# A graph-attention kernel: edge gates transposed on VectorE in 32x32 blocks, bands of 1024 rows, all adjacency loads from SyncE

## The chip, the core and the metric

The kernel runs on one core of one Trainium2 chip. Its time is the device time of one execution in microseconds (us), the median of three runs. The core has TensorE (PE in the profile; PEld is its weight load), VectorE (DVE), ScalarE (ACT), GpSimd (POOL) and SyncE (SP), which here only issues transfers. A transfer (DMA) runs on the core's 16 DMA engines.

## The reference

One layer of graph attention over N = 8192 nodes with 128 features. The adjacency matrix is 8192 x 8192 int32, 268.4 MB, and is by far the largest input.

```
h = max(layernorm(x), 0);  Wh = h @ W
s1 = Wh @ a[:128];  s2 = Wh @ a[128:]
e = leaky_relu(s1[:, None] + s2[None, :], 0.2)
attention = softmax(where(adj > 0, e, -9e15), axis=1)
out = x + elu(attention @ Wh)
```

## The kernel before

**Stages.** A first stage loads x, normalises it, and builds `wh`: for each of 64 column tiles of 128 nodes, 128 partitions by 130 columns (the features, a one for the row sum, s1). Then the main loop goes over 16 bands of 512 rows. With a row factor and a column factor the softmax weight of row i and column j is `min(max(rbc[i], beta[j]), gate[i, j])`, where the gate byte is 1 for an edge and 0 for none, and a factor of the column is already multiplied into `wh`. This is the path that is taken when the spread of the scores is small (`safe_path`); the other path doesn't run on these inputs.

**One chunk** is 512 rows by 1024 columns, 2 MB of `adj`; there are 8 in a band and 128 in all. SP loads it with one transfer (`load`, L192) into one of 4 slots of `raw`: 128 partitions, 4 rows to a partition, runs of 4 KB. It may start when ScalarE has read the chunk that was in the slot (`gate_ready`). ScalarE turns it into bytes with `Sign` (`form_gates`, L407) into one of 2 slots of `gate`. TensorE transposes the gates, since the products need columns on the partitions: 16 transposes of 128x128 two-byte words into PSUM (`turn_gates`, L804). VectorE forms the weights for one column tile and 512 rows with one instruction (`steps`, L623), 8 to a chunk, reading the gate bytes from PSUM, into one of 4 slots of `weights`. TensorE multiplies (`multiply`, L814): 4 products of 128x128 by 128x129 in float32 to a step, each of which the trace shows as two passes; 4096 products, 8192 passes in all.

**Order.** Each engine has its own program, and they meet on semaphores. TensorE's program puts the transposes of the next chunk behind the fourth step of a chunk (`TURN_STEP`), in the same stream as the products. VectorE may be 4 steps ahead of TensorE (`weights_used`). The sums of a band are copied by ScalarE in the middle of the next band (L412), finished on GpSimd (L293 to L305, with one `Exp` on ScalarE), and stored by GpSimd's own queue (L307). For the next band TensorE spreads s1 over the partitions (`turn_s1`, L785) and VectorE and ScalarE make `rbc` (L572, L422). The last band is finished on VectorE (`last_band`) and stored by SP.

Of the kernel before, what the change touches and what calls it, by code (L numbers as in the profile page):

```python
# [13 lines left out]
P = 128  # L31
# [3 lines left out]
SAFE_SPREAD = 60.0  # L35

QUAD = 4
PACK = 2
ROWS = QUAD
CHUNK = 1024  # L40
STEPS = CHUNK // P
RAW_SLOTS = 4
GATE_SLOTS = 2
TURNED_SLOTS = 4
WT_SLOTS = 4
GROUP = QUAD
DVE_TILES = (1, 1, 2, 2)


def graph_attention(nc, x, adj, w, a, out):  # L50
    N, F = x.shape
    NT = N // P
    BANDS = N // (ROWS * P)
    BAND = ROWS * P
    CHUNKS = N // CHUNK
    GROUPS = NT // GROUP
# [5 lines left out]
    TURN_STEP = STEPS // 2 - 1  # L62
# [3 lines left out]
    QUADS = CHUNK // (QUAD * P)  # L66
    GATHER = QUAD
    assert F == P and CHUNKS % RAW_SLOTS == 0 and QUAD % WT_SLOTS == 0 and BANDS % 2 == 0
    assert len(DVE_TILES) == PER_PART

    with ExitStack() as ctx:
# [3 lines left out]
        def sem(name):  # L75
            return ctx.enter_context(nc.semaphore(name))

        raw = sb("raw", [P, RAW_SLOTS, ROWS, CHUNK], I32)
        gate = sb("gate", [P, GATE_SLOTS, ROWS, CHUNK], U8)
        xs = sb("xs", [P, NT, F])  # L80
        rbc = sb("rbc", [P, 2, BAND])
        wh = sb("wh", [P, NT, FE])
        s1_band = sb("s1_band", [P, ROWS])
        s2_all = sb("s2_all", [P, N])
        weights = sb("weights", [P, WT_SLOTS, BAND])
        hacc = sb("hacc", [P, 2, ROWS, FD])
        obuf = sb("obuf", [P, 2, ROWS, F])
        hp = sb("hp", [P, ROWS, F])
        neg = sb("neg", [P, ROWS, F])

        xn = weights[:, 0:2, :].rearrange("p s (t f) -> p s t f", f=F)
        ht = weights[:, 2:4, :]
        identf = sb("identf", [P, P])
        identb = sb("identb", [P, P], BF16)
        zeros = sb("zeros", [P, 2 * FD], BF16)
# [19 lines left out]
        empty = sb("empty", [P, 2, ROWS])  # L115
        rden = sb("rden", [P, 2, ROWS])
# [3 lines left out]
        acc = [ps[:, 2 * k:2 * k + 2, 0:2 * FD] for k in range(2)]  # L120
        wh_acc = [ps[:, 2 * k:2 * k + 2, 0:2 * FE] for k in range(2)]

        turned = [ps[:, 4 + k, :].bitcast(BF16).rearrange("p (c i) -> p c i", i=BAND) for k in range(TURNED_SLOTS)]
        turned_bytes = [ps[:, 4 + k, :].bitcast(U8).rearrange("p (c i b) -> p c i b", i=BAND, b=PACK)
                        for k in range(TURNED_SLOTS)]

        w_in, a_in = sem("w_in"), sem("a_in")  # L130
        x_in = [sem(f"x_in{k}") for k in range(4)]
        raw_in = [sem(f"raw_in{k}") for k in range(RAW_SLOTS)]
        out_done = [sem(f"out_done{k}") for k in range(2)]
# [9 lines left out]
        hmean_ready, mwh_done, mwh_ready = sem("hmean_ready"), sem("mwh_done"), sem("mwh_ready")  # L143
        ext_ready, gext_ready, flag_ready = sem("ext_ready"), sem("gext_ready"), sem("flag_ready")
        bias_ready = sem("bias_ready")

        s1_ready, s1_turned = sem("s1_ready"), sem("s1_turned")
        d_ready, z_ready, r_ready = sem("d_ready"), sem("z_ready"), sem("r_ready")
        w_first, w_rest = sem("w_first"), sem("w_rest")
        gate_ready = sem("gate_ready")  # L150
        turned_ready = sem("turned_ready")
        weights_ready = sem("weights_ready")
        weights_used = sem("weights_used")

        sums_copied = sem("sums_copied")
        hacc_free = sem("hacc_free")
        last_neg, last_exp, last_ready, last_out = (
            sem("last_neg"), sem("last_exp"), sem("last_ready"), sem("last_out"))
        rden_ready, neg_ready, exp_ready, out_ready = (
            sem("rden_ready"), sem("neg_ready"), sem("exp_ready"), sem("out_ready"))  # L160
# [3 lines left out]
        g_scores, g_probs = sem("g_scores"), sem("g_probs")  # L164
        g_turned, g_copied, g_used = sem("g_turned"), sem("g_copied"), sem("g_used")

        scores = raw[:, 2:4, :, :].rearrange("p s t j -> p (s t j)").bitcast(F32)
        adj_rows = raw[:, 0:2, :, :].rearrange("p s t j -> p (s t j)")
        x_blocks = x.rearrange("(k p b) f -> p k b f", p=P, b=QUAD)
        adj_blocks = adj.rearrange("(k p b) j -> p k b j", p=P, b=QUAD)  # L170
        out_blocks = out.rearrange("(k p b) f -> p k b f", p=P, b=QUAD)
# [9 lines left out]
        def _(sp):  # L181

# [3 lines left out]
            for load_of_x, (lo, hi) in enumerate([(0, PART // 2), (PART // 2, PART), (PART, 2 * PART), (2 * PART, NT)]):  # L186
                sp.dma_start(xs[:, lo:hi, :].rearrange("p (k b) f -> p k b f", b=QUAD),
                             x_blocks[:, lo // QUAD:hi // QUAD, :, :]).then_inc(x_in[load_of_x], 16)

            def load(band, chunk, slot):  # L190
                rows = adj_blocks[:, bass.ds(band, 1), :, chunk * CHUNK:(chunk + 1) * CHUNK]
                sp.dma_start(raw[:, slot, :, :], rows.rearrange("p k b j -> p (k b) j")).then_inc(raw_in[slot], 16)  # L192

            for k in range(RAW_SLOTS):
                load(0, k, k)

            def safe_path():

                for k in range(RAW_SLOTS, CHUNKS):
                    sp.wait_ge(gate_ready, k - RAW_SLOTS + 1)  # L200
                    load(0, k, k % RAW_SLOTS)
                with sp.Fori(1, BANDS) as band:
                    for k in range(CHUNKS):
                        sp.wait_ge(gate_ready, band * CHUNKS + (k - RAW_SLOTS + 1))
                        load(band, k, k % RAW_SLOTS)
                sp.wait_ge(last_ready, 1)
                sp.dma_start(out_blocks[:, BANDS - 1, :, :],
                             weights[:, 2, :].rearrange("p (b f) -> p b f", f=F)).then_inc(last_out, 16)
                sp.wait_ge(last_out, 16)

            def general_path():

                sp.wait_ge(gate_ready, 1)
                for k in range(RAW_SLOTS):
                    sp.wait_ge(raw_in[k], 16)
                with sp.Fori(0, BANDS) as k:
                    for b in range(QUAD):
                        sp.wait_ge(g_adj_free, k * QUAD + (b + 1))
                        sp.dma_start(adj_rows, adj_blocks[:, bass.ds(k, 1), b, :].rearrange("p k j -> p (k j)"))\
                            .then_inc(g_adj, 16)  # L220
# [10 lines left out]
        def _(pool):  # L231
            links = [0]

            def link(ins):

                links[0] += 1
                ins.then_inc(pool_chain, 1)
                pool.wait_ge(pool_chain, links[0])


            pool.sem_inc(hacc_free, 2)
            link(nc.gpsimd.memset(identf[:, :], 0.0))
            link(nc.gpsimd.affine_select(out=identf[:, :], in_=identf[:, :], compare_op=ALU.not_equal, fill=1.0,
                                         base=0, pattern=[[-1, P]], channel_multiplier=1))
            nc.gpsimd.tensor_copy(identb[:, :], identf[:, :]).then_inc(consts, 1)
            nc.gpsimd.memset(zeros[:, :], 0.0).then_inc(consts, 1)
            pool.sem_inc(consts, 1)
# [30 lines left out]
            LINKS = 4  # L278
            base = links[0]

            def finish_band(band, half, tiles, first, to, stored=None):

                done = [0]

                def chained(ins):
                    done[0] += 1
                    ins.then_inc(pool_chain, 1)
                    pool.wait_ge(pool_chain, band * LINKS + (base + done[0]))

                h, n, o = hp[:, 0:tiles, :], neg[:, 0:tiles, :], obuf[:, half, 0:tiles, :]  # L290
                row = [P, tiles, F]
                pool.wait_ge(rden_ready, band + 1)
                nc.gpsimd.tensor_tensor(n, empty[:, half, 0:tiles].unsqueeze(2).to_broadcast(row),  # L293
                                        mean_wh[:, :].unsqueeze(1).to_broadcast(row), ALU.mult)
                chained(nc.gpsimd.tensor_tensor(h, hacc[:, half, 0:tiles, 0:F],  # L295
                                                rden[:, half, 0:tiles].unsqueeze(2).to_broadcast(row), ALU.mult))
                chained(nc.gpsimd.tensor_tensor(h, h, n, ALU.add))  # L297
                pool.sem_inc(hacc_free, 1)
                nc.gpsimd.tensor_scalar(n, h, 0.0, None, ALU.min).then_inc(neg_ready, 1)  # L299
                chained(nc.gpsimd.tensor_scalar(h, h, 0.0, -1.0, ALU.max, ALU.add))  # L300
                if stored is not None:
                    pool.wait_ge(out_done[half], stored * 16)
# [6 lines left out]
            def finish_bands():  # L309
                def rows(band):  # L310
                    return out_blocks[:, bass.ds(band, 1), :, :].rearrange("p k b f -> p (k b) f")
# [607 lines left out]
```

## Time and profile before

| what | us |
|---|---|
| median of 3 runs (1108.24 to 1108.91) | 1108.8 |
| span of the profiled execution | 1107.6 |
| TensorE busy | 1077.9 |
| VectorE busy | 814.1 |
| ScalarE busy | 510.1 |
| GpSimd busy | 186.1 |

The span goes from the first to the last instruction of the profiled execution; a run's time has a little more around it. Busy time of matmuls is modelled, since they are pipelined; what a stretch of them costs is better read from the distance between their starts.

### The profile page before, as it was taken

To read this page: it belongs to the slowest core of one execution; us is meant where nothing else is said; L and a number is where in the kernel's file an instruction comes from. 1 tells how busy PE (TensorE), PEld (TensorE's weight loads), DVE (VectorE), ACT (ScalarE), POOL (GpSimd) and SP (SyncE) were. 2 spreads that over 40 slices of the span, in tenths; PEclk is the share of its full clock that TensorE was granted. 3 is DMA by queue.
4 is the path that set the end of the run, shared out by engine and by line. 5 is a ranking of instruction groups with operands and counts; after the bars stand their busy time and mean duration, and the time that the engine had idled before them with its cause. 6 is when DMAs were issued, how large, how long until landed. Compare 5 with 4: busy or idle time off the path is not lost.

```text
span 1107.6 us, 27993 instructions
## 1 busy us (share of the span) xinstructions
PE 1077.9 (97%) x10533; PEld 1072.1 (97%) x10533; DVE 814.1 (73%) x1249; ACT 510.1 (46%) x234; POOL 186.1 (17%) x168
## 2 busy tenths in 40 slices
PE   4799999999999999999999999999999999999997
PEld 4699999999999999999999999999999999999997
DVE  7677777777777777777777777777777777777776
ACT  3845435354453544544445444544454353544440
POOL 4340020110302012030200303020030202103030
PEclk9899999999999999999999999999999999999999
DMA  9596776776676767767677676676767767666700
GB/s 331 198 350 230 272 275 253 262 277 234 234 300 249 288 232 270 267 227 300 240 273 266 240 280 247 264 276 240 272 230 282 273 247 269 270 238 232 299 9 14
DMA packets 71499, 277.24 MB, mean 250 GB/s; under 512 B 2672, under 2 KB 2800, under 8 KB 71472
## 3 DMA queue, kind: packets, MB, share of 16 engines
q1 hardware_dynamic: 70272, 272.97, 64.9%
q0 software_dynamic: 1200, 3.93, 0.9%
q8 instruction: 15, 0.25, 0.1%
q14 instruction: 12, 0.10, 0.0%
HBM read 272.70 MB, written 4.19 MB: 250 GB/s over the span
## 4 chain that ended last, share of the span: by engine, by line
PE 94%; DVE 3%; issue 1%; DMA 0%; POOL 0%; POOLq 0%; ACT 0%; SPq 0%; DVEq 0%
PE ps L814 83%; PE ps L804 10%; DVE stats L490 1%; DVE weights L524 1%; PE ps L785 1%; PE ps L762 0%; PE ps L755 0%; DMA xs<-in_x 0%; PE ps L823 0%; DVE mean L507 0%; POOL wh L341 0%; DVE tmp L509 0%; DVE mean L505 0%; DVE weights L647 0%; DVE weights L642 0%
## 5 line engine op out<-in xcount | busy, mean ns | idle before, releaser
L623 DVE SCALAR_TENSOR_TENSOR weights<-rbc,beta,ps 128x512 f32<-128x512 f32 x1024 | 760.7, 747 | 271.0 <-PE ps L814 162.7
L814 PE MATMUL ps<-wh,weights 128*128 (+1 forms) x8192 | 949.8, 276 | 1.2 <-DVE weights L623 0.9
L814 PEld LDWEIGHTS ps<-wh,weights 128*128 128x128 f32 x8192 | 929.2, 192 | 2.1 <-issue 1.9
L407 ACT ACTIVATE gate<-raw 128x4096 uint8<-128x4096 int32 x127 | 459.0, 3615 | 442.5 <-PE ps L804 442.5
L804 PE MATMUL ps<-identb,gate 128*128 128x128 bf16 x2048 | 136.0, 220 | 1.8 <-DVE mean_wh L593 1.8
L293 POOL TENSOR_TENSOR neg<-empty,mean_wh 128x512 f32<-128x512 f32 x15 | 15.5, 1031 | 703.3 <-DVE rden L606 703.3
L804 PEld LDWEIGHTS ps<-identb,gate 128*128 128x128 bf16 x2048 | 125.9, 98 | 3.8 <-DVE mean_wh L593 2.2
L422 ACT ACTIVATE rbc<-rbc 128x512 f32<-128x512 f32 x16 | 10.1, 630 | 103.3 <-DVE rbc L572 103.3
L305 POOL TENSOR_TENSOR obuf<-obuf,neg 128x512 f32<-128x512 f32 x15 | 19.2, 1278 | 136.3 <-ACT neg L417 136.3
L300 POOL TENSOR_SCALAR hp<-hp 128x512 f32<-128x512 f32 x15 | 28.9, 1925 | 0.0
L755 PE MATMUL ps<-identf,weights 128*128 128x128 f32 x64 | 11.2, 302 | 13.5 <-POOL weights L262 9.5
L299 POOL TENSOR_SCALAR neg<-hp 128x512 f32<-128x512 f32 x15 | 22.5, 1500 | 3.1 <-POOL hp L297 3.1
L755 PEld LDWEIGHTS ps<-identf,weights 128*128 128x128 f32 x64 | 7.7, 154 | 15.6 <-issue 9.5
L303 POOL TENSOR_TENSOR obuf<-hp,xs 128x512 f32<-128x512 f32 x15 | 19.1, 1274 | 3.1 <-POOL hp L300 2.9
L297 POOL TENSOR_TENSOR hp<-hp,neg 128x512 f32<-128x512 f32 x15 | 19.1, 1270 | 1.2
L762 PE MATMUL ps<-wext,weights 128*128 128x130 f32 x128 | 17.8, 285 | 0.0
L762 PEld LDWEIGHTS ps<-wext,weights 128*128 128x128 f32 x128 | 16.4, 200 | 0.1
L341 POOL TENSOR_TENSOR wh<-wh,dcol x7 | 13.2, 1890 | 14.0 <-issue 13.7
L295 POOL TENSOR_TENSOR hp<-hacc,rden 128x512 f32<-128x512 f32 x15 | 15.5, 1031 | 0.0
L490 DVE BATCH_NORM_STATS2 stats<-xs 128x6 f32<-128x128 f32 x64 | 13.1, 280 | 2.3 <-DMA xs<-in_x 2.3
L259 POOL TENSOR_TENSOR weights<-xs,mean 128x384 f32 (+3 forms) x16 | 11.7, 730 | 13.6 <-DVEq L518 11.6
L447 ACT ACTIVATE weights<-weights 128x512 f32<-128x512 f32 x1 | 0.6, 630 | 26.8 <-DVE weights L650 26.8
(68 smaller groups left out, 151.6 us busy)
## 6 DMA issues: line engine op xcount, KB each, us to landing
raw<-in_adj SPq DMA_DIRECT2D x128, 2048.0 KB, 7.7
out_x<-obuf POOLq DMA_DIRECT2D x15, 256.0 KB, 2.4
xs<-in_x SPq DMA_DIRECT2D x1, 2048.0 KB, 12.9
xs<-in_x SPq DMA_DIRECT2D x2, 512.0 KB, 4.1
xs<-in_x SPq DMA_DIRECT2D x1, 1024.0 KB, 7.5
out_x<-weights SPq DMA_DIRECT2D x1, 256.0 KB, 2.2
wext<-in_L_gnn_W SPq DMA_DIRECT2D x1, 64.0 KB, 1.9
a<-in_L_gnn_a SPq DMA_DIRECT2D x2, 0.5 KB, 2.0
```

The lines of the kernel that those rows point to most:

```text
L297: chained(nc.gpsimd.tensor_tensor(h, h, n, ALU.add))
L299: nc.gpsimd.tensor_scalar(n, h, 0.0, None, ALU.min).then_inc(neg_ready, 1)
L300: chained(nc.gpsimd.tensor_scalar(h, h, 0.0, -1.0, ALU.max, ALU.add))
L303: chained(nc.gpsimd.tensor_tensor(o, h, xs[:, bass.ds(first, tiles), :], ALU.add))
L305: nc.gpsimd.tensor_tensor(o, o, n, ALU.add).then_inc(out_ready, 1)
L407: nc.scalar.activation(gate[:, k % GATE_SLOTS, :, :], raw[:, k % RAW_SLOTS, :, :], ACT.Sign).then_inc(gate_ready, 1)
L490: ins = nc.vector.bn_stats(stats[:, t, :].rearrange("p t s -> p (t s)"), xs[:, t, :].rearrange("p t s -> p (t s)"))
L623: nc.vector.scalar_tensor_tensor(weights[:, u % WT_SLOTS, :], rbc[:, half, :], beta[:, bass.ds(jt, 1)], turned_bytes[u // QUAD % TURNED_SL ...
L755: ins = nc.tensor.transpose(ps[:, 4 + slot, u * P:(u + 1) * P], xn[:, slot, u, :], identf[:, :])
L762: ins = nc.tensor.matmul(wh_acc[slot][:, u // 2, (u % 2) * FE:(u % 2 + 1) * FE], ht[:, slot, u * P:(u + 1) * P], wext[:, :], start=True, s ...
L804: ins = nc.tensor.transpose(turned[(k * QUADS + q) % TURNED_SLOTS][:, c, r * P:(r + 1) * P], words[:, c, :], identb[:, :])
L814: ins = nc.tensor.matmul(acc[half][:, r // 2, (r % 2) * FD:(r % 2 + 1) * FD], weights[:, u % WT_SLOTS, r * P:(r + 1) * P], wh[:, bass.ds(p ...
```

## The change

The gates are no longer transposed on TensorE. VectorE transposes them in blocks of 32x32 four-byte words, from SBUF to SBUF. A block transpose moves nothing between groups of 32 partitions, so the load has to put the rows and columns where the blocks need them.

- A band has 1024 rows (8 bands), a chunk is 1024 rows by 1024 columns (4 MB, 64 in all), loaded as two units of 2 MB (`load_unit`): 16 units in a band, 128 in all. The 4 slots of `raw` hold a unit each.
- A unit is loaded by four transfers of 512 KB, one for each group of 32 partitions, in the order 0, 2, 1, 3. Each partition takes 16 runs of 256 words (1 KB). `x` is loaded the same way, by 32 transfers (8 x 4) in place of 4. SP issues all of them.
- VectorE transposes a unit with one instruction of 128x1024 words, 2 in a chunk, behind its steps 3 and 6 and for the chunk that follows. A step forms 128x1024 weights, reads the gate bytes from SBUF, and multiplies by them instead of taking the minimum. TensorE has 8 products in a step.
- `rbc` is made from the transposed rows by ScalarE straight out of PSUM; `turn_z` takes the place of `turn_s1`. The share of rows without an edge comes in by three small bf16 products a band (`add_mean`).
- The sums are scaled by ScalarE from PSUM (`take_sums`: 16 small activations a band), finished on VectorE (`elu`, three instructions of 128x1024), and stored by SP, whose program waits for them between the loads of units 10 and 11 of the next band. GpSimd has no part in it any more.

```diff
-ROWS = QUAD
-CHUNK = 1024
+SQ = 32
+RUN = 256
+WORDS = RUN // QUAD
+WB = WORDS // SQ
+CHUNK = 4 * RUN
 STEPS = CHUNK // P
+BAND = CHUNK
+TILES = BAND // P
+UNIT = BAND // 2
+BLOCKS = UNIT // SQ
 RAW_SLOTS = 4
 GATE_SLOTS = 2
-TURNED_SLOTS = 4
...
+        g_o = [obuf[:, k * F:(k + 1) * F] for k in range(2)]
+
+
+        x_runs = x.rearrange("(k a w y b) f -> a k y w (b f)", a=4, w=WB, y=SQ, b=QUAD)
+        out_runs = out.rearrange("(k a w y b) f -> a y k w (b f)", a=4, w=WB, y=SQ, b=QUAD)
+
+        adj_runs = adj.rearrange("(k q w x b) j -> w x b k q j", q=4, w=WB, x=SQ, b=QUAD)
+        adj_tiles = adj.rearrange("(k a w y b) j -> a w b y k j", a=4, w=WB, y=SQ, b=QUAD)
+
+        def load_x(eng, k, group):
+            part = slice(group * SQ, (group + 1) * SQ)
+            eng.dma_start(xs[part, k * STEPS:(k + 1) * STEPS, :].rearrange("p (w b) f -> p w (b f)", b=QUAD),
+                          x_runs[group, k]).then_inc(x_in[k], 16)
+
+        def load_unit(eng, band, unit, groups):
+            chunk, half = unit // 2, unit % 2
+            slot = unit % RAW_SLOTS
+            for group in groups:
+                first = chunk * CHUNK + group * RUN
+                rows = adj_runs[half][:, :, bass.ds(band, 1), :, first:first + RUN]
+                eng.dma_start(raw[group * SQ:(group + 1) * SQ, slot, :, :].rearrange("p (b q) j -> p b q j", q=4),
+                              rows.rearrange("x b k q j -> x b (k q) j")).then_inc(raw_in[slot], 16)
...
+            for k in range(CHUNKS):
+                for group in (0, 2, 1, 3):
+                    load_x(sp, k, group)
+            for u in range(RAW_SLOTS):
+                load_unit(sp, 0, u, (0, 2, 1, 3))
...
+                    load_unit(sp, 0, u, (0, 2, 1, 3))
                 with sp.Fori(1, BANDS) as band:
-                    for k in range(CHUNKS):
-                        sp.wait_ge(gate_ready, band * CHUNKS + (k - RAW_SLOTS + 1))
-                        load(band, k, k % RAW_SLOTS)
-                sp.wait_ge(last_ready, 1)
-                sp.dma_start(out_blocks[:, BANDS - 1, :, :],
-                             weights[:, 2, :].rearrange("p (b f) -> p b f", f=F)).then_inc(last_out, 16)
-                sp.wait_ge(last_out, 16)
+                    for u in range(UNITS):
+                        sp.wait_ge(gate_ready, band * UNITS + (u - RAW_SLOTS + 1))
+                        load_unit(sp, band, u, (0, 2, 1, 3))
+                        if u == UNITS - 6:
+                            sp.wait_ge(out_ready, band)
+                            store_band(sp, band - 1, range(4), out_done)
+                for h in range(2):
...
+                def form_gates(band, u):
+                    turn = u // RAW_SLOTS + 1
+                    act.wait_ge(raw_in[u % RAW_SLOTS], band * (UNITS // RAW_SLOTS * 64) + turn * 64)
+                    if not isinstance(band, int) or band * UNITS + u >= GATE_SLOTS:
+                        act.wait_ge(turned_ready, band * UNITS + (u - GATE_SLOTS + 1))
+                    nc.scalar.activation(gate[:, u % GATE_SLOTS, :, :], raw[:, u % RAW_SLOTS, :, :], ACT.Sign)\
+                        .then_inc(gate_ready, 1)
...
                 def exp_rows(band, half):
-
-                    act.wait_ge(z_ready, band + 1)
-                    nc.scalar.activation(rbc[:, half, :], rbc[:, half, :], ACT.Exp, scale=SLOPE - 1.0)\
-                        .then_inc(r_ready, 1)
+                    act.wait_ge(z_turned, band + 1)
+                    nc.scalar.activation(rbc[:, half, :], zps.rearrange("p b i -> p (b i)"), ACT.Exp,
+                                         scale=SLOPE - 1.0).then_inc(r_ready, 1)
+
+                def take_sums(band, half):
+                    act.wait_ge(rden_ready, band + 1)
+                    if not isinstance(band, int) or band >= 1:
+                        act.wait_ge(out_ready, band)
+                    for t in range(TILES):
+                        rows, columns = slice(t * F, (t + 1) * F), acc[half][:, t // BANK_TILES, t % BANK_TILES, 0:F]
+                        scale = rden[:, half, t // BANK_TILES, t % BANK_TILES:t % BANK_TILES + 1]
+                        nc.scalar.activation(hbuf[:, rows], columns, ACT.Copy, scale=scale)
+                        ins = nc.scalar.activation(ebuf[:, rows], columns, ACT.Exp, scale=scale)
+                    ins.then_inc(sums_taken, 1)
+
+                def band_of_gates(band, half, first=False, last=False):
+                    for u in range(first, UNITS):
+                        form_gates(band, u)
+                        if u == 7 and not first:
+                            take_sums(band - 1, 1 - half)
+                        if u == 13 and not last:
+                            exp_rows(band + 1, 1 - half)
...
+                def turn_gates(band, u):
+                    dve.wait_ge(gate_ready, band * UNITS + (u + 1))
+                    words = gate[:, u % GATE_SLOTS, :, :].bitcast(I32).rearrange("p k (w y) -> p w k y", w=WB)
+                    half = u % 2
+                    nc.vector.transpose(turned[:, u // 2 % 2, :, half * UNIT:(half + 1) * UNIT], words)\
+                        .then_inc(turned_ready, 1)
+
+                def steps(band, half, pair, last=False):
+                    for u in range(PAIR):
+                        jt = pair * PAIR + u
+                        chunk, v = u // STEPS, u % STEPS
+                        if v == 0:
+                            dve.wait_ge(turned_ready, band * UNITS + pair * 4 + (2 * chunk + 2))
+                        dve.wait_ge(weights_used, band * BAND_STEPS + (jt + 1))
+                        nc.vector.scalar_tensor_tensor(
+                            weights[:, u % WT_SLOTS, :], rbc[:, half, :], beta[:, bass.ds(jt, 1)],
+                            turned_bytes[:, chunk, v // QUAD, :, v % QUAD], ALU.max, ALU.mult)\
+                            .then_inc(weights_ready, 1)
+                        if v in (3, 6) and not (last and chunk == 1):
+
+                            ahead = 2 * chunk + 1 + v // 3
+                            dve.wait_ge(gate_ready, band * UNITS + pair * 4 + (ahead + 1))
+                            words = gate[:, ahead % GATE_SLOTS, :, :].bitcast(I32)\
+                                .rearrange("p k (w y) -> p w k y", w=WB)
+                            to = slice((v // 3 - 1) * UNIT, v // 3 * UNIT)
+                            nc.vector.transpose(turned[:, 1 - chunk, :, to], words).then_inc(turned_ready, 1)
+
+                def reciprocals(band, half):
+
+                    dve.wait_ge(weights_used, band * BAND_STEPS + (BAND_STEPS + WT_SLOTS))
+                    nc.vector.reciprocal(rden[:, half, :, :], acc[half][:, :, :, F]).then_inc(rden_ready, 1)
+
+                def elu(band):
+                    def chained(k, ins):
+                        ins.then_inc(elu_chain, 1)
+                        dve.wait_ge(elu_chain, band * 2 + k)
+
+                    dve.wait_ge(sums_taken, band + 1)
+                    chained(1, nc.vector.tensor_scalar(ebuf, ebuf, 1.0, -1.0, ALU.min, ALU.add))
+                    chained(2, nc.vector.tensor_tensor(ebuf, ebuf, hbuf, ALU.max))
+                    if not isinstance(band, int) or band >= 1:
+                        dve.wait_ge(out_done, band * 64)
+                    nc.vector.tensor_tensor(
+                        obuf[:, :], ebuf, xs[:, bass.ds(band * TILES, TILES), :].rearrange("p t f -> p (t f)"), ALU.add)\
+                        .then_inc(out_ready, 1)
+
+                def band_of_weights(band, half, first=False, last=False):
+                    dve.wait_ge(r_ready, band + 1)
+                    if not last:
+                        z_of_band(band + 1)
+                    steps(band, half, 0)
+                    if not first:
+                        reciprocals(band - 1, 1 - half)
+                    steps(band, half, 1)
+                    if not first:
+                        elu(band - 1)
+                    if last:
+                        for pair in range(2, PAIRS):
+                            steps(band, half, pair, last=pair == PAIRS - 1)
+                    else:
+                        with dve.Fori(2, PAIRS) as pair:
+                            steps(band, half, pair)
...
+                def chunk_of_products(band, chunk, half, start=False, stop=False):
+                    pe.wait_ge(w_rest, chunk + 1)
+                    for u in range(STEPS):
+                        multiply(band, chunk, u, half, start and u == 0, stop and u == STEPS - 1)
+
...
+                def band_of_products(band, half, last=False, wait=True):
+                    if wait:
+                        pe.wait_ge(sums_taken, band - 1)
+                    chunk_of_products(band, 0, half, start=True)
+                    with pe.Fori(1, TURN_CHUNK) as chunk:
+                        chunk_of_products(band, chunk, half)
                     if not last:
-                        pe.wait_ge(sums_copied, band + 2)
-                        turn_s1(band + 1, 1 - half)
-                    with pe.Fori(PAIRS // 2, PAIRS - last) as pair:
-                        pair_of_chunks(pair)
-                    if last:
-                        for u in range(PAIR):
-                            if u == TURN_STEP:
-                                turn_gates(band, PAIRS - 1, 1)
```

## Rows read from the trace of the kernel before

**Rows 1.** The page: span, busy time and share of the engines
```profile
span 1107.6 us, 27993 instructions
PE 1077.9 (97%) x10533; PEld 1072.1 (97%) x10533; DVE 814.1 (73%) x1249; ACT 510.1 (46%) x234; POOL 186.1 (17%) x168
PE 94%; DVE 3%; issue 1%; DMA 0%; POOL 0%; POOLq 0%; ACT 0%; SPq 0%; DVEq 0%
```

**Rows 2.** Groups by line and shape: busy us, mean ns, idle before and releaser
```profile
L814 PE MATMUL ps<-wh,weights 128*128 x7936 | 920.5, 276 | 1.2 <-DVE weights L623 0.9 <-POOL wh L341 0.4
...
L804 PE MATMUL ps<-identb,gate 128*128 128x128 bf16 x2048 | 136.0, 220 | 1.8 <-DVE mean_wh L593 1.8
```

**Rows 3.** Chain that ended last: start us, length us, what
```profile
450.80 7.20 PE ps L814 x64
458.90 7.20 PE ps L814 x64
...
516.22 7.20 PE ps L814 x64
...
1088.09 11.68 PE ps L814 x104
```

**Rows 4.** Waits: who, for whom, us in total, times, longest
```profile
ACT gate L407 <- PE ps L804: 442.5, 110, 5.1
DVE weights L623 <- PE ps L814: 162.7, 192, 1.1
```

**Rows 5.** Groups by line and shape, VectorE and ScalarE
```profile
L623 DVE SCALAR_TENSOR_TENSOR weights<-rbc,beta,ps 128x512 f32<-128x512 f32 x1024 | 760.7, 747 | 271.0 <-PE ps L814 162.7 <-PE ps L804 0.8
L407 ACT ACTIVATE gate<-raw 128x4096 uint8<-128x4096 int32 x127 | 459.0, 3615 | 442.5 <-PE ps L804 442.5
...
L412 ACT COPY hacc<-ps 128x516 f32<-128x516 f32 x15 | 8.5, 570 | 0.0
...
L611 DVE TENSOR_TENSOR wh<-wh,dcol 128x1024 f32<-128x1024 f32 x1 | 1.2, 1226 | 0.2 <-issue 0.2
...
L642 DVE TENSOR_SCALAR weights<-ps,tmp 128x128 f32<-128x128 f32 x4 | 1.1, 346 | 0.0
...
L655 DVE SCALAR_TENSOR_TENSOR weights<-weights 128x512 f32<-128x512 f32 x1 | 0.7, 693 | 0.2 <-ACT weights L447 0.2
...
L650 DVE TENSOR_SCALAR weights<-weights 128x512 f32<-128x512 f32 x1 | 0.4, 427 | 0.0
```

**Rows 6.** Timeline where the main loop starts: start us, length us
```profile
47.49 0.15 DVE L590 TENSOR_SCALAR flag<-spread 128x1 int32<-128x1 f32 x1
...
50.90 2.72 DVE L623 SCALAR_TENSOR_TENSOR weights<-rbc,beta,ps 128x512 f32<-128x512 f32 x4 [0.81 <-PE ps L804]
```

**Rows 7.** Timeline of the end
```profile
1099.80 0.16 DVE L638 TENSOR_SCALAR tmp<-ps 128x4 f32<-128x4 f32 x1 [2.83 <-PE ps L814]
...
1104.66 0.37 SPq L207 DMA_DIRECT2D out_x<-weights  x1
```

**Rows 8.** The adjacency loads by line: issue ns (min/median/max), landing us
```profile
L192 SPq DMA_DIRECT2D raw<-in_adj x128: 539/543/5507, 4.3 to 1043.4; - x128
...
DMA to landing us min/median/max: 7.5/7.7/24.9
```

**Rows 9.** DMA in 20 to 34 us, 12 to 14 us and 4 to 10 us
```profile
DMA packets 1447, 5.73 MB, mean 410 GB/s; under 512 B 48, under 2 KB 48, under 8 KB 1446
...
DMA packets 400, 0.82 MB, mean 410 GB/s; under 512 B 0, under 2 KB 0, under 8 KB 400
...
DMA packets 1017, 2.01 MB, mean 334 GB/s; under 512 B 38, under 2 KB 38, under 8 KB 1017
```

More of the change, by code:

```diff
@@ L167, in graph_attention @@
+        adj_rows = raw[:, 0:2, :, :].rearrange("p s t j -> p (s t j)")
         scores = raw[:, 2:4, :, :].rearrange("p s t j -> p (s t j)").bitcast(F32)
[L168 to L171, printed above, removed]
+        g_hacc = [weights[:, k, UNIT:UNIT + FD] for k in range(2)]
@@ L173, in safe, with store_band @@
+        def store_band(eng, band, groups, signal):
+            for group in groups:
+                part = slice(group * SQ, (group + 1) * SQ)
+                rows = out_runs[group][:, bass.ds(band, 1), :, :].rearrange("y k w c -> y (k w) c")
+                eng.dma_start(rows, obuf[part, :].rearrange("p (w c) -> p w c", w=WB)).then_inc(signal, 16)
         def safe(eng):
@@ L276, in _ @@
                 .then_inc(gext_ready, 1)
-            LINKS = 4
             base = links[0]
[L281 to L302, printed above, removed]
-                chained(nc.gpsimd.tensor_tensor(o, h, xs[:, bass.ds(first, tiles), :], ALU.add))
-                pool.wait_ge(exp_ready, band + 1)
-                nc.gpsimd.tensor_tensor(o, o, n, ALU.add).then_inc(out_ready, 1)
-                pool.wait_ge(out_ready, band + 1)
-                pool.dma_start(to, o).then_inc(out_done[half], 16)
@@ L672, in safe_path @@
-                band_of_weights(0, 0)
+                for u in range(2):
+                    turn_gates(0, u)
+                band_of_weights(0, 0, first=True)
                 band_of_weights(1, 1)
@@ L845, in safe_path, with multiply @@
-                turn_gates(0, 0, 0)
+                def multiply(band, chunk, u, half, start, stop):
+                    pe.wait_ge(weights_ready, band * BAND_STEPS + chunk * STEPS + (u + 1))
+                    moving = wh[:, bass.ds(chunk * STEPS + u, 1), 0:FD].rearrange("p t f -> p (t f)")
+                    for t in range(TILES):
+                        ins = nc.tensor.matmul(acc[half][:, t // BANK_TILES, t % BANK_TILES, 0:FD],
+                                               weights[:, u % WT_SLOTS, t * P:(t + 1) * P], moving,
+                                               start=start and t % BANK_TILES == 0, stop=stop, skip_group_check=True)
+                    ins.then_inc(weights_used, 1)
@@ new lines, in band_of_products @@
+                def band_of_products(band, half, last=False, wait=True):
[4 more added lines that the diff above has]
+                        chunk_of_products(band, chunk, half)
+                    if not last:
+                        pe.wait_ge(r_ready, band + 1)
+                        turn_z(band + 1)
+                    with pe.Fori(TURN_CHUNK, CHUNKS - 1) as chunk:
+                        chunk_of_products(band, chunk, half)
+                    add_mean(half)
+                    chunk_of_products(band, CHUNKS - 1, half, stop=True)
@@ L846, in safe_path @@
                 pe.wait_ge(w_first, 2)
-                with pe.Fori(0, BANDS // 2 - 1) as pair:
+                for half in range(2):
+                    band_of_products(half, half, wait=False)
+                with pe.Fori(1, BANDS // 2 - 1) as pair:
                     for half in range(2):
```

480 lines of the change are left out of this document (212 added, 268 removed).

## The prediction

> **What bounds the kernel now.** I read the shares first: TensorE is busy 97% of the span and takes 94% of the chain that ended last, VectorE 73% [rows 1]. Of TensorE's time 8192 passes are products and 2048 are gate transposes; its waits for weights come to 1.2 us in all [rows 2]. VectorE and ScalarE wait for TensorE, 162.7 and 442.5 us [rows 4]. So TensorE's instruction stream is the limit, and the reader sees there what a chunk costs. The chain has a stretch of 64 passes every 8.09 us (450.80 to 458.90); the 64 take 7.20 us, 112.5 ns a pass, and the 16 transposes add 0.89 us, not the 1.06 that their busy time says. At the end 104 passes with no transpose among them take 11.68 us, 112.3 ns each, so the price holds without transposes too. A band takes 65.42 us (450.80 to 516.22), eight chunks and 0.70 us of its own [rows 3]. The loads are hidden: 2 MB land 7.7 us after issue [rows 8], and at 410 GB/s [rows 9] they occupy the DMA engines for 5.1 of the 8.09 us.
>
> **The change part by part.** The sum is made against the span, 1107.6 us; the median of the runs is 1.2 above it.
>
> TensorE. 128 times 16 transposes go: 128 x 0.89 = 114 us off the path. The passes stay 8192. The spreading of the row scores stays 64 transposes; 32 zeroing products become 24 wider ones. I count the 0.70 us of a band as unchanged for the same rows: 0. What is left is 7.20 us per 2 MB unit.
>
> VectorE is no longer covered as well. A step of 1024 columns from SBUF: the same operation took 693 ns for 512 columns, and 1024 columns of a two-input operation took 1226 ns [rows 5]; I take 1.23. No block transpose is in the trace. Bounds for 128x1024 words: twice the 427 ns of a one-input operation of 512 columns, 0.85 us, below, and two passes of the two-input one, 2.46 us, above; I take 1.23, the row with the same number of elements. A chunk is then 8 + 2 instructions, 12.3 us, against 14.4 us of products. `elu` adds 3 x about 1.1 us a band, which the four weight slots (up to 5 us of products ahead) cover. Nothing on the path. (The Trainium skill, page Vector Engine (DVE) Microarchitecture Reference, section 3.8 on the reshape front-end, has the block transpose sustain one element per cycle per lane; at its 0.96 GHz that would be 1.07 us plus a fixed part, and the sum would be the same. No run here shows it yet.)
>
> ScalarE: 16 gates of 3.62 us a band [rows 5], 16 activations of 128 columns (under 0.57 us each, the price of 516 columns), one `Exp` of 1024: under 69 of 115 us. Off the path.
>
> Start. Before, the first weights came 3.4 us after the flag, on one chunk's gates made in advance [rows 6]. Now the first step needs two units, and ScalarE makes the second after the flag (3.62 us), then VectorE transposes it: +4 us (0 to +10). End: last product to store issue took 4.9 us [rows 7]. Now 8 scalings at 0.28 to 0.35 us and two halves of three operations follow, and the store is split: +2 us.
>
> SP's program. `store_band` waits for `out_ready` between the loads of units 10 and 11, and loads 11 to 15 are queued behind it. `out_ready` comes after step 31 and `elu`. With VectorE three steps ahead and a step of 1.8 us, step 31 ends at 52 us of the band and `elu` at 55.6. Load 10 was issued when the gate of unit 6 was formed, at about 20.5 (unit 4 is transposed behind step 11, at 16.9, and the gate takes 3.6), so the DMA engines have nothing for 30 us. Four stores take 4 x 0.54 us to issue, load 11 goes out at 57.7, lands at 65.4, its gate is ready at 69.0, and its transpose was due behind step 38 at 64.2. Three steps of reserve cover all but 1 to 2 us; seven bands: +10 us (5 to 25).
>
> The loads. This decides. A unit is 2 MB in 7.20 us: 291 GB/s are wanted. The trace shows 410 GB/s, 25.6 per engine, at 4 KB packets and also at 2 KB packets, 334 where half-megabyte transfers follow each other [rows 9], always with all 128 partitions as the destination. That the rate doesn't depend on the packet says that each engine is held by a path in bytes. If the path is the engine's own, 32 partitions cost nothing: 410 is the bound above. If it belongs to the partitions, a transfer to 32 of them has its 16 engines, two partitions each, meet on fewer paths: half, 205 GB/s, is the bound that I take below. A second reason gives the same bound: should a 1 KB packet take the 80 ns that a 2 KB packet takes (400 in 2 us on 16 engines), the rate is 205 too. Groups 0 and 2 alternate, so engines that have drifted apart use different paths; but all start a transfer together and share evenly, and nothing drives them apart. I take 230, the lower bound and an eighth for such overlap.
>
> At 230 GB/s the loads set the end. x, `adj` and seven stored bands are 4.2 + 268.4 + 3.7 = 276.3 MB: 1201 us, starting at 4. Since DMA never idles in the first stage (12.6 MB are queued before the flag at 47.5), the gap before the main loop is used up. In each of seven bands the wait of SP for `out_ready` leaves the queue dry: after load 9 lands, 3.6 (gate) + 1.2 + 1.2 + 3.4 (transpose, step 31, `elu`) + 2.1 (stores) + 2 to the first byte is 13.5 us, against 9.1 for load 10: 4 x 7 = 28. After the last landing: gate 3.6, transpose 1.2, eight steps of products 14.4, end 10: 29. Together 4 + 1201 + 28 + 29 = 1262, with 1.2 around the span **1263 us**.
>
> The Trainium skill, page SBUF — State Buffer, section Door 1 (the DMA port swizzle), says that partitions 0 to 31 reach 8 of 16 ports, 189 GB/s at 1 MB against 328 for all partitions, 218 at best; its part on issuing two DMAs for both halves says that they serialize, 6% better than one. By 218 the sum would be 1329, by 6% more, 231 GB/s, 1258. No transfer of before goes to fewer partitions, so the trace can't say whether it agrees.
>
> **The rivals.**
> *Full rate.* The path is the engine's own and 1 KB packets cost by their bytes. For it: the same 25.6 GB/s per engine at two packet sizes. Against: no row with few partitions. At 334 GB/s or more a unit takes 6.3 us or less, under 7.20, TensorE stays the limit: 1107.6 - 114 + 4 + 2 + 10 = 1010, with 1.2 **1011 us** (995 to 1040). Faster. It decides from 291 GB/s up; between that and 264 the change still gains.
> *Partly shared.* The pairs drift apart by half a transfer: 410/1.5 = 273 GB/s, 276.3 MB in 1012 us, with 61 us around: 1074. For it: twelve hundred microseconds are long to drift. Against: engines that run dry start together again. Break-even is at 264 GB/s (1047 us of transfers).
> *VectorE becomes the bound.* The transpose takes the 2.46 us of its upper bound: a chunk is 8 x 1.23 + 4.92 = 14.8 against 14.4 us; with 3.7 us a band for `elu` and the sums, 64 x 14.8 + 8 x 3.7 = 977 in place of 922 + 6: at full rate 1011 + 50 = 1061. Against: 1.23 has the nearest row, and TensorE's stretch gives it 2 us a chunk of slack.
>
> **How the numbers follow.** Loads at 205 to 264 GB/s, 52%: 1110 to 1409 by the bounds, its own range 1120 to 1400, 1263 likeliest. Full rate 33%. Partly shared, about 255 to 291 GB/s, 11%: 6 faster, 2 within the bound, 3 slower. VectorE 4%. Faster by over 0.2% (about what a measurement of this kernel tells from no change): 33 + 4 + 6 = 43%. Within 0.2%: 2%. Slower: 52 + 3 = 55%. The range for 8 in 10 has to hold both signs: 1003 to 1385.
>
> **What would show it.** Right: TensorE's busy share falls to about 75%, the chain goes through DMA landings and ScalarE's gate, ScalarE's idle time is put down to `raw`, the DMA share is near 1.0 in nearly all slices while GB/s are near 230, and a packet of 1 KB takes 70 ns or more. Wrong: GB/s above 290 where loads are dense, a packet of 42 ns or less, TensorE at 7.20 us for 64 passes without gaps. The steps on SP: SP waits for VectorE's last `elu` instruction seven times, with no DMA in that time. The transpose of 128x1024 at 1.2 us; the step at 1.23; the first weights 7 us behind the flag. If VectorE is busy over 95% while TensorE waits for weights, it is the third rival.

## The result: 19% slower, and the loads set the time

The changed kernel takes 1319.5 us (median of 4 runs, 1313.2 to 1324.0) against 1108.9 us (4 runs, 1108.2 to 1109.8) before. The ratio is 1.190 with a 95% interval of 1.186 to 1.193. The forecast was 1263 us, by the case in which the loads become the limit; its own range was 1120 to 1400. The page and rows below are of the run of 1313.2 us.

The page of the changed kernel, to be read against [rows 1]: span, busy time, the clock, DMA and GB/s in 40 slices, and the chain that ended last by engine.

```profile
span 1311.6 us, 21997 instructions
PE 1049.4 (80%) x8477; PEld 1026.5 (78%) x8477; DVE 843.5 (64%) x825; ACT 523.8 (40%) x309; POOL 55.9 (4%) x63
...
DMA  8999999999999999999999999999999999999990
GB/s 222 223 225 222 223 223 221 220 197 216 215 218 217 202 223 223 221 223 196 218 219 217 205 211 221 221 220 198 223 224 225 223 200 222 222 222 222 200 207 18
...
q1 hardware_dynamic: 275760, 276.67, 106.1%
...
SPq 75%; DMA 9%; issue 6%; DVE 5%; ACT 3%; PE 2%; DVEq 0%; POOL 0%; ACTq 0%
```

TensorE fell from 97% busy to 80% and from 94% of the chain to 2%. The DMA engines are busy in every slice but the last and still move only 196 to 225 GB/s, where [rows 9] had 410. They are not idle, their packets are slow: 106.1% of 16 x 1311.6 us over 275,760 packets is 81 ns for one of 1 KB (a share above 100% says that the times of an engine's packets overlap a little).

The waits (engine, line, for whom: us in total, times, longest) answer to [rows 4].

```profile
ACT gate L409 <- DMA raw<-in_adj: 735.5, 125, 11.6
DVE big L604 <- ACT gate L409: 414.1, 111, 9.2
PE ps L801 <- DVE weights L593: 224.3, 88, 7.3
...
SPq L183 <- DVE obuf L621: 80.7, 7, 11.8
```

ScalarE waited for TensorE's transposes before; now it waits for a landing at 125 of its 127 gates, VectorE's transposes wait for ScalarE, TensorE waits for VectorE. The last line is SP waiting for the band's result, once in each of seven bands.

ScalarE's gates in order of time (start, length, what, idle before) show the pace of the units and one wait of SP. The last line below is the window around that wait (us, busy time of the engines, then the clock, the DMA share and GB/s).

```profile
745.14 3.62 ACT L409 ACTIVATE gate<-raw 128x4096 uint8<-128x4096 int32 x1 [6.04 <-DMA raw<-in_adj]
754.49 3.62 ACT L409 ACTIVATE gate<-raw 128x4096 uint8<-128x4096 int32 x1 [5.73 <-DMA raw<-in_adj]
768.94 3.62 ACT L409 ACTIVATE gate<-raw 128x4096 uint8<-128x4096 int32 x1 [10.83 <-DMA raw<-in_adj]
...
750.00:759.00 9.00, 5.62 (x48) 5.25 (x47) 8.80 (x9) 3.62 (x1) 0.00 (x0) 1.00 0.60 134
```

Between waits a gate follows the last one after 9.3 to 9.8 us in most cases (9.35 in the lines shown); a unit of 2.097 MB in 9.6 us is 218 GB/s, in 9.35 it is 224. Where SP waited the distance is 14.45 us, 4.8 to 5.1 more. Not all of that is lost: the band's store, 0.52 MB, falls into it. In the 9 us around the wait the DMA engines moved 134 GB/s, which at a pace of 221 is 3.5 us without work.

The compute side is as the forecast had it. These are the groups by line (busy us, mean ns, idle before).

```profile
L593 DVE SCALAR_TENSOR_TENSOR weights<-big,beta 128x1024 f32<-128x1024 f32 x512 | 634.1, 1289 | 23.7 <-PE ps L801 23.4
L604 DVE STREAM_TRANSPOSE big<-gate 128x1024 int32<-128x1024 int32 x126 | 156.8, 1244 | 414.2 <-ACT gate L409 414.1
```

### The profile page after: what moved, and what is told of

Read it like the earlier page. It is cut to its first block, busy times and chain, and to the rows that moved or that the text cites. A ratio compares the mean times of both kernels' runs of the same rounds, so it can differ in the third digit from the quotient of the medians.

```text
span 1311.6 us, 21997 instructions
## 1 busy us (share of the span) xinstructions
PE 1049.4 (80%) x8477; PEld 1026.5 (78%) x8477; DVE 843.5 (64%) x825; ACT 523.8 (40%) x309; POOL 55.9 (4%) x63
## 3 DMA queue, kind: packets, MB, share of 16 engines
q1 hardware_dynamic: 275760, 276.67, 106.1%
## 4 chain that ended last, share of the span: by engine, by line
SPq 75%; DMA 9%; issue 6%; DVE 5%; ACT 3%; PE 2%; DVEq 0%; POOL 0%; ACTq 0%
SPq L176 74%; DMA raw<-in_adj 8%; ACT gate L409 3%; PE ps L801 1%; SPq L183 1%; DVE stats L497 1%; DVE weights L593 1%; DVE big L618 1%; DVE obuf L621 1%; DVE weights L527 1%; DVE big L617 0%; PE ps L767 0%; DVE big L604 0%; DMA xs<-in_x 0%; SPq L208 0%
## 5 line engine op out<-in xcount | busy, mean ns | idle before, releaser
L801 PE MATMUL ps<-wh,weights 128*128 (+1 forms) x8192 | 1008.3, 288 | 231.7 <-DVE weights L593 224.3
L801 PEld LDWEIGHTS ps<-wh,weights 128*128 128x128 f32 x8192 | 990.0, 203 | 249.8 <-issue 198.2
L593 DVE SCALAR_TENSOR_TENSOR weights<-big,beta 128x1024 f32<-128x1024 f32 x512 | 634.1, 1289 | 23.7 <-PE ps L801 23.4
L604 DVE STREAM_TRANSPOSE big<-gate 128x1024 int32<-128x1024 int32 x126 | 156.8, 1244 | 414.2 <-ACT gate L409 414.1
L425 ACT ACTIVATE big<-ps,rden 128x128 f32<-128x128 f32 x56 | 23.3, 417 | 0.0
L424 ACT ACTIVATE big<-ps,rden 128x128 f32<-128x128 f32 x56 | 22.9, 409 | 0.0
L788 PE MATMUL ps<-identf,zband 128*128 128x128 f32 x64 | 12.4, 360 | 0.8 <-DVE zband L566 0.8
L387 ACT ACTIVATE weights<-ps 128x512 f32<-128x512 f32 x16 | 9.6, 598 | 6.3 <-PE ps L760 6.3
L527 DVE TENSOR_SCALAR weights<-xs,mean,rstd 128x128 f32<-128x128 f32 x24 | 10.2, 463 | 2.8 <-PE ps L760 2.8
L788 PEld LDWEIGHTS ps<-identf,zband 128*128 128x128 f32 x64 | 11.0, 191 | 1.0 <-DVE zband L566 1.0
L267 POOL TENSOR_TENSOR weights<-weights,rstd 128x384 f32<-128x384 f32 (+1 forms) x16 | 11.6, 725 | 2.2 <-POOL weights L264 1.4
```

Of the source, the lines that this page charges most:

```text
L424: nc.scalar.activation(hbuf[:, rows], columns, ACT.Copy, scale=scale)
L425: ins = nc.scalar.activation(ebuf[:, rows], columns, ACT.Exp, scale=scale)
L527: ins = nc.vector.tensor_scalar(xn[:, slot, u, :], xs[:, t, :], mean[:, t:t + 1], rstd[:, t:t + 1], ALU.subtract, ALU.mult)
L593: nc.vector.scalar_tensor_tensor(weights[:, u % WT_SLOTS, :], rbc[:, half, :], beta[:, bass.ds(jt, 1)], turned_bytes[:, chunk, v // QUAD, ...
L604: nc.vector.transpose(turned[:, 1 - chunk, :, to], words).then_inc(turned_ready, 1)
L788: ins = nc.tensor.transpose(zps[:, t // 4, t % 4 * P:(t % 4 + 1) * P], zband[:, t:t + 1].to_broadcast([P, P]), identf[:, :])
```

## The experiments

**Is it the 32 partitions? Two loads for the kernel before.** The first loads each chunk by four transfers of 32 neighbouring partitions, the second by four transfers of 32 partitions that lie four apart. All else is equal between them: the number and size of the transfers, packets of 4 KB, and how many partitions a transfer has. (The semaphore counts change to 64 to match; so in all runs with four transfers.)

```diff
-                sp.dma_start(raw[:, slot, :, :], rows.rearrange("p k b j -> p (k b) j")).then_inc(raw_in[slot], 16)
+                for group in (0, 2, 1, 3):                            # second run: range(4)
+                    part = slice(group * 32, (group + 1) * 32)        # second run: slice(group, P, 4)
+                    sp.dma_start(raw[part, slot, :, :], rows[part].rearrange("p k b j -> p (k b) j"))\
+                        .then_inc(raw_in[slot], 16)
```

> The kernel before, but each 2 MB chunk is loaded by four transfers of 32 neighbouring partitions in the order 0, 2, 1, 3, still in packets of 4 KB. Theory A (write paths belong to partitions, 32 neighbours reach half of them): 218 GB/s in dense stretches, 9.6 us a chunk against TensorE's 8.09, so the loads become the limit: about 14 + 128 x 9.6 + 12 = 1255 us. Theory B (a 1 KB packet costs nearly what a 2 KB packet costs): packets are 4 KB here, nothing changes, 1109. Theory C (transfers of 512 KB are too small): 334 GB/s or what the change showed, 218; by the former 1109, by the latter 1255, and then the next run tells it from A.

> As the run before, but each of the four transfers goes to 32 partitions four apart (0, 4, 8 ... then 1, 5, 9 ...). Same number of transfers, sizes, packets and partitions per transfer. Theory A: these 32 reach all write paths, 400 GB/s or more where loads are dense, 1109 us. Theory B: 1109. Theory C (size or number of transfers): the same time as the run with neighbouring partitions, 1255 if that one is slow.

Measured: 1237.8 us with neighbours, 1108.9 us with every fourth (before on the same chip: 1108.6; one run each). The page of the first and then of the second:

```profile
GB/s 255 226 228 229 229 234 225 225 233 224 233 225 225 231 223 231 225 225 232 224 233 225 233 224 224 232 224 232 225 225 233 225 233 226 233 225 228 237 231 41
...
q1 hardware_dynamic: 76416, 272.99, 99.5%
```

```profile
q1 hardware_dynamic: 76416, 272.99, 69.0%
```

Where the loads are dense at the start, from 20 to 34 us, the second moves 410 GB/s as the kernel before does [rows 9], and the first 224:

```profile
20.00:34.00 14.00, 10.31 (x85) 9.28 (x84) 13.47 (x54) 11.35 (x27) 10.32 (x15) 1.00 1.03 410
```

The same 76,416 packets take 257 ns each to neighbours (99.5% of 16 x 1236.1 us) and 160 ns to every fourth partition (69.0% of 16 x 1107.2). So neither the number of partitions nor the size of a transfer costs anything here; which partitions they are does. That is theory A: the limit in bytes belongs to groups of partitions, and 32 neighbours get little more than half of the full rate. The Trainium skill, page SBUF — State Buffer, section Door 1 (the DMA port swizzle), gives 8 of 16 ports and at best 218 GB/s for partitions 0 to 31. The traces agree on the half, but not on "at best": the changed kernel moves 215 to 225 GB/s in slices without a store, and this run 223 to 237 from its second slice on (the stores, 1.4% of the bytes, are in it). With the groups in the order 0, 1, 2, 3 it is 209 to 220 (the fifth experiment).

**Is it the 1 KB packet?** The kernel before with four transfers a chunk of all 128 partitions, each for 256 columns, so in packets of 1 KB. (A version with one transfer a chunk and 1 KB runs gave no result.)

```diff
+                for c in range(4):
+                    first = chunk * CHUNK + c * 256
+                    rows = adj_blocks[:, bass.ds(band, 1), :, first:first + 256]
+                    sp.dma_start(raw[:, slot, :, c * 256:(c + 1) * 256], rows.rearrange("p k b j -> p (k b) j"))\
+                        .then_inc(raw_in[slot], 16)
```

> The kernel before, each 2 MB chunk in four transfers of 128 partitions, one for each quarter of the columns: four transfers of 512 KB and packets of 1 KB, as in the changed kernel, but every transfer goes to all partitions. Theory A (write paths of the 32 partitions): 350 to 400 GB/s where loads are dense, a packet of 1 KB takes 41 to 47 ns, hidden behind TensorE, 1109 us, at most 1115. Theory B (cost of the 1 KB packet, or of 1 KB reads at the memory): 205 to 230 GB/s, 9.1 to 10.2 us a chunk, 1200 to 1330 us.

Measured: 1108.7 us against 1109.0. From its page, and its window from 20 to 34 us:

```profile
q1 hardware_dynamic: 273024, 272.99, 75.6%
...
20.00:34.00 14.00, 10.41 (x85) 9.38 (x84) 13.57 (x56) 11.44 (x27) 10.61 (x16) 1.00 1.10 349
```

A packet took 49 ns (75.6% of 16 x 1107.0 us over 273,024), against 81 in the changed kernel. A quarter of the length costs 0.31 of the 160 ns above: by a straight line through the two, an estimate, the fixed part is some 12 ns. It isn't free, since the dense stretch has 349 GB/s in place of 410, but it is far from the half, and theory B falls. The memory's layout is not the same here (rows 32 KB apart in turn, not also 8 MB apart), so for that part only the next run speaks.

**Are both halves of the paths free at once?** The changed kernel, with the transfers to partitions 64 to 127 of the main loop issued by ScalarE's queue as soon as it has freed the slot.

```diff
-                        load_unit(sp, band, u, (0, 2, 1, 3))
+                        load_unit(sp, band, u, (0, 1))
...
+                def load_ahead(band, u):
+                    act.wait_ge(gate_ready, band * UNITS + (u + 1))
+                    load_unit(act, band + (u + RAW_SLOTS) // UNITS, (u + RAW_SLOTS) % UNITS, (2, 3))
...
                         form_gates(band, u)
+                        if not (last and u + RAW_SLOTS >= UNITS):
+                            load_ahead(band, u)
...
+                load_ahead(0, 0)
```

> The changed kernel, but SP issues only the transfers to partitions 0 to 63 in the main loop, and ScalarE's queue those to 64 to 127 for the same unit. Theory A with engines that take packets from both queues in turn: both halves of the write paths are in use at once, 300 to 400 GB/s, TensorE is the limit again: 1010 to 1060 us. Theory A with engines that finish one queue's transfer first, and theory B: 218 GB/s as in the changed kernel, about 1310.

Measured: 1022.3 us against 1108.6 (one run), faster than either kernel. From the page and, last, SP's waits:

```profile
GB/s 221 218 301 348 329 290 294 299 215 181 329 347 347 189 245 344 346 308 179 297 346 311 235 176 317 346 347 206 229 346 346 320 179 287 346 347 238 197 113 23
...
SPq L183 <- DVE obuf L628: 229.2, 7, 34.0
```

The same bytes, packets, addresses and partitions as in the changed kernel, now at up to 348 GB/s, so the memory isn't what held them. That is also what packets of 1 KB reach when every transfer goes to all partitions (349). The first two slices are 221 and 218: there SP still issues all four groups alone. TensorE is busy 94% of the span, so the other slices show what is asked for and not always what is possible. What no run separates is the second queue itself from its going to the other half: two queues to the same 64 partitions were not tried.

The Trainium skill says otherwise: page DMA: Bandwidth & Descriptors, section Issuing engines are not separate DMA queues, has several issuing engines save only the issue time, and page SBUF — State Buffer, section "Can I just issue two DMAs to hit both halves?", measured 6%. Here the second queue brings 222 to 347 GB/s in dense slices, 56%; the measurement decides.

**Does the order 0, 2, 1, 3 help in one queue?** The changed kernel with `(0, 2, 1, 3)` replaced by `(0, 1, 2, 3)` in its four places.

> The changed kernel with its transfers in the order 0, 1, 2, 3, so that groups on the same half of the paths follow each other. If the engines are in step within a transfer, as I now think, the order 0, 2, 1, 3 gains nothing from its alternation: 9.6 us a unit and 1310 to 1325 us here too. If the alternation does give overlap at each change of group, this one is slower: 5% less rate would be 1380 us.

Measured: 1352.7 us (one run), 2.5% over the changed kernel and 29 us above the slowest of its four runs, with 209 to 220 GB/s in the slices without a store against 215 to 225. So alternation buys a little, 3 to 4% of the rate, between my two cases. That it comes from the moments at which one transfer hands over to the next is my reading; no view shows it.

**What is SP's wait worth?** Two ways to take it away in the changed kernel, loads untouched: the stores on GpSimd's queue (with a semaphore of their own), or still on SP but behind the load of unit 15, where the result has long been there.

```diff
# stores by GpSimd
-                        if u == UNITS - 6:
-                            sp.wait_ge(out_ready, band)
-                            store_band(sp, band - 1, range(4), out_done)
...
+                with pool.Fori(1, BANDS) as band:
+                    pool.wait_ge(out_ready, band)
+                    store_band(pool, band - 1, range(4), out_soft)
```

```diff
# stores late on SP
-                        if u == UNITS - 6:
+                        if u == UNITS - 1:
                             sp.wait_ge(out_ready, band)
                             store_band(sp, band - 1, range(4), out_done)
```

> The changed kernel with the seven band stores issued by GpSimd's queue in place of SP's program; the loads stay as they are. If SP's wait for the band's result is what leaves the DMA engines dry once a band (one gate interval of 14.45 us in place of 9.62), this takes 7 x 4.8 = 34 us away: 1285 us. If the gap is the stores themselves on the DMA engines (0.5 MB at 218 GB/s is 2.4 us), at most 17 us stay and the gain is 17: 1302.

> The changed kernel with its band stores still issued by SP, but behind the load of unit 15 in place of unit 10, where the band's result has long been there, so SP doesn't wait. With the stores on GpSimd's queue the time was 1182, 103 us under what the gap of 7 x 4.8 us explains (1285), and the rate rose from 225 to 250 GB/s and more from about 430 us on. Theory D1: engines that never run dry drift apart by themselves, and each dry spell had put them in step again: then this one shows the same, 1150 to 1230 us, with rates that rise in the course of the run. Theory D2: the packets of GpSimd's queue pushed single engines out of step: then the rate here stays at 218 to 225, with 1280 to 1295 us.

Measured: 1182.4 us (one run) for GpSimd, and 1167.2 and 1233.2 us (two runs, the trace is of the first) for the late store. My 1285 was missed by 100 us. GB/s in 40 slices, for the store by GpSimd and for the late store:

```profile
GB/s 222 222 223 225 225 226 226 226 225 238 226 224 223 223 239 230 230 229 244 276 288 266 273 286 253 254 258 238 257 243 234 248 270 269 255 241 239 241 173 20
```

```profile
GB/s 222 222 225 226 225 226 225 224 224 227 235 234 235 242 282 310 284 255 232 233 236 227 226 228 226 236 226 228 237 276 254 235 277 288 283 294 266 266 211 21
```

For the first 265 to 290 us both run at 222 to 227 as the changed kernel does between its waits. Then the rate wanders: up to 310, back to 226, up to 294. Since it does so without GpSimd's queue as well, theory D2 falls. D1 has the course of the rate right, and 1167 is in its range, but 1233 is just outside. In the changed kernel the queue runs dry once a band, every 158 us, and its slices never exceed 225. That the engines drift apart within a transfer and are put in step again by a dry spell is my reading of this; no view shows the single engines, and one run speaks against it as a general rule. The first experiment, 32 neighbouring partitions in packets of 4 KB, has SP never waiting longer than 4.1 us, transfers that land 25.5 us after issue because others are queued ahead, and stores on GpSimd's queue; yet it stays at 223 to 237 GB/s from the second slice to the end of its loads. So a queue that never runs dry isn't enough. What else it takes (the 1 KB packet, the layout) is open, and so is why the second run of the late store was 66 us longer.

**The version that beats both.** Two queues for the loads, and no wait of SP: stores on GpSimd's queue, or late on SP.

> Both: loads from SP and ScalarE's queue, stores from GpSimd's. TensorE is the limit, and what is left of SP's wait in the two-queue kernel (a gap of 1.5 us in TensorE's products in most bands, with ScalarE waiting up to 17 us for a load) goes: 1022 - 7 x 1.5 = 1012 us. If the stores from GpSimd disturb the loads or VectorE's steps with two inputs in SBUF, the gain is smaller: 1015 to 1025.

> The two-queue kernel with SP's stores behind the load of unit 15. If SP's wait was the only rest beside TensorE, this equals the two-queue kernel with stores from GpSimd: 1009 +- 3 us. If the stores of 32 partitions in SP's own queue hold up the loads behind them, 1012 to 1020. Should GpSimd's software queue have cost something there, it is 1005 to 1008.

Measured: 1009.4 us (4 runs, 1009.0 to 1012.1; ratio to before 0.910, interval 0.909 to 0.912) and 1009.9 us (4 runs, 1009.2 to 1011.2; ratio 0.911, interval 0.910 to 0.913). Who issues the stores makes no difference. TensorE's timeline of the late-store version:

```profile
340.20 57.34 PE L808 MATMUL ps<-wh,weights 128*128 x512
```

512 passes in 57.34 us are 112.0 ns each, the price of [rows 3]: TensorE is the limit again, without transposes. The full-rate case of the prediction had 1011, with 10 us for SP's wait in it.

## Why the prediction was right

*TensorE.* 7.20 us for 64 passes was right: 7.17 in the last run. The 114 us are real; in the changed kernel they don't show because TensorE waits.

*VectorE.* The transpose took 1.24 us (taken: 1.23, from a two-input operation of as many elements). The step took 1.29 where I had 1.23, 5% more than the row of 1024 elements that I took it from. A chunk is 12.8 us of 14.4, still hidden; the third rival is out.

*Start and end.* The first weights came 7.6 us after the flag (48.38 to 56.00), forecast 7. From the last landing to the end of the span it was 34 us, forecast 29. The timeline of that end:

```profile
1277.58 3.62 ACT L409 ACTIVATE gate<-raw 128x4096 uint8<-128x4096 int32 x1 [5.74 <-DMA raw<-in_adj]
...
1283.79 3.47 PE L801 MATMUL ps<-wh,weights 128*128 x16 [3.73 <-DVE weights L593]
...
1287.82 14.46 PE L801 MATMUL ps<-wh,weights 128*128 128x129 f32 x128
```

Eight steps behind the last gate are 14.46 us as counted. Left out was that TensorE still had a step of the chunk before to do, which came late too (16 passes that end at 1287).

*SP's wait.* 4 us a band forecast, 28 in all, beside the stores, whose bytes are in the 276.3 MB. Windows of 9 us around the seven waits moved 130 to 149 GB/s; at a pace of 221 they lack 24 us in all, 3.4 a band. (The 4.8 us by which the gates lie further apart hold the store as well.) As a gap it was sized about right. But taking it away gave 137 us (the store by GpSimd) and 152 and 86 us (the late store), since in the two runs with a trace the loads then left the half level.

*The loads.* The mis-sized term: 230 GB/s, the bound of 205 and an eighth for overlap. With 4 us ahead, 24 of gaps and 34 behind the last landing, 1250 of the 1311.6 us are left for 276.3 MB: 221 GB/s. So the loads took 49 us more than forecast, the end 5 more and the gaps 4 less, which makes the 50 us between forecast and span. The bound was somewhat low and the allowance too large: without alternation the rate is about 214, and the alternation of the groups brings 3 to 4%, not an eighth. Two errors of opposite sign, and the 230 came out nearer than its working deserved.

The first reason given for the bound, that 32 partitions get half the paths, is borne out by the first two runs as far as the rate goes. The second, a 1 KB packet that takes as long as one of 2 KB, is wrong: 49 ns to all partitions. The sign "70 ns or more" came true with 81 ns, but it holds under both reasons and could not tell them apart. That nothing drives the engines apart held in this kernel, where SP waits once a band; without the wait the rate did leave the half level. The rival of partly shared paths (273 GB/s) is not what this kernel does, nor, on average, what it does once SP no longer waits: 235 and 238 GB/s over the span, with slices up to 310. The full-rate rival fell for one queue; with a second queue 1009 us were measured. That this lies within 2 us of its 1011 is partly luck: the 1011 hold 10 us for SP's wait, and with two queues and that wait it was 1022.

## What to carry to other kernels

Before a layout that needs loads into 32 neighbouring partitions at a time, price the load at about half the rate of a full one, 215 to 225 GB/s in place of 410, and ask what hides it: here the hidden 5.1 us of 2 MB became 9.5 against 7.2 of products. If the layout is worth it, issue the lower and the upper 64 partitions from two queues at the same time: 347 GB/s, enough to turn +19% into -8%, and -9% with SP's wait gone as well. And keep a wait for a result out of the program that issues the loads, or put it where the result is long there; here, with the loads as the limit, it cost more than its own length.

## What I had not expected of the hardware

The rate of a load stream to 32 neighbouring partitions at a time is not always a constant: in 1 KB packets, with the queue never dry, it wandered between 222 and 310 GB/s in one run and between 222 and 288 in another; in 4 KB packets it stayed at 223 to 237.

VectorE's steps now have two inputs in SBUF, and while GpSimd scales `wh` in the first 20 us of the main loop, both slow down. The groups and the timeline of the changed kernel:

```profile
L308 POOL TENSOR_TENSOR wh<-wh,dcol x7 | 18.4, 2633 | 9.8 <-issue 9.5
```

```profile
56.00 9.79 DVE L593 SCALAR_TENSOR_TENSOR weights<-big,beta 128x1024 f32<-128x1024 f32 x4
...
66.88 7.43 DVE L593 SCALAR_TENSOR_TENSOR weights<-big,beta 128x1024 f32<-128x1024 f32 x3
```

These steps take 2.4 to 2.5 us each in place of 1.29, and GpSimd's operation 2.63 us where the same one took 1.89 in the kernel before. Before, the gate bytes came from PSUM. The Trainium skill, page SBUF — State Buffer, section Who interferes with whom, has a VectorE instruction with two SBUF inputs contend with a GpSimd instruction that reads SBUF; by that rule, the trace agrees, though no run here took the overlap away. Seven steps at 1.2 us more are some 8 us of VectorE's time at the start, an estimate from these lines; how much of it the kernel would get back is not shown.
